# A three-layer decoder on one core: orders of latent values and context, a second bank for values, and layer 2's first steps moved into layer 1

## The reference, cut to what matters

```python
# layer 1: local attention of 16 heads of 16 (keys strictly before the query) and latent attention of 4 heads
local  = softmax(mask(q @ k.T / 4)) @ v                    # q, k, v = split(xn @ qkv_w + qkv_b)
pooled = xn.reshape(B, 64, 2, D).mean(axis=2)              # 64 latent tokens
lat    = softmax(mask(rq @ rk.T / 4)) @ rv                 # rq = xn @ rq_w + rq_b; rk, rv from pooled
remote = lat @ rout_w + rout_b
gate   = sigmoid(local @ gl_w + remote @ gr_w)             # per head
x      = x + (gate * local + (1 - gate) * remote) @ out_w + out_b
# layer 2: causal attention of x on a context
q, k, v = relu(xn @ Wq + bq), relu(ctx @ Wk + bk), relu(ctx @ Wv + bv)
x      = x + layer_norm(softmax(mask(q @ k.T / 4)) @ v + q, gamma, beta)
# layer 3: a slot feed-forward (routing to 64 slots, top 8, one GRU step, values given back)
```

## Time and profile before

| | us |
|---|---|
| median of three runs | 1517.61 |
| lowest and highest of them | 1512.31, 1517.75 |
| profiled execution | 1513.51 |
| its span | 1511.8 |

### The profile page before, as it was taken

One profiled execution on the slowest core, in us unless ns is written; L12 is line 12 of the kernel. 1 busy time (PEld: TensorE's weight loads), 2 busy tenths in 40 slices (PEclk: granted clock), 3 DMA queues, 4 the chain that ended last, 5 costly groups with the idle time before them and its releaser, 6 DMA issues. The chain is left out here.

```text
span 1511.8 us, 57218 instructions
## 1 busy us (share of the span) xinstructions
PE 1416.7 (94%) x22238; PEld 1064.8 (70%) x22238; DVE 1101.2 (73%) x3030; ACT 888.3 (59%) x1541; POOL 873.5 (58%) x1184
## 2 busy tenths in 40 slices
PE   6999999999999999985999999999999859999997
PEld 4777777777777777764777777777777636666664
DVE  6777777777777777653667676767676658989896
ACT  3555555555555555542666666666667347777773
POOL 3455555555555555542577777777777635555543
PEclk9999999999999999998999999999999969999998
DMA  5400000000000000003000000000000000010101
GB/s 165 135 2 1 0 0 0 0 0 0 0 0 0 0 0 0 2 3 120 17 24 14 21 14 21 14 21 14 21 14 8 2 1 29 29 35 28 35 28 42
DMA packets 31207, 32.40 MB, mean 21 GB/s; under 512 B 3937, under 2 KB 29602, under 8 KB 31138
## 3 DMA queue, kind: packets, MB, share of 16 engines
q1 hardware_dynamic: 31138, 31.46, 6.9%
HBM read 23.06 MB, written 8.39 MB: 21 GB/s over the span
## 5 line engine op out<-in xcount | busy, mean ns | idle before, releaser
L1028 POOL TENSOR_SCALAR_AFFINE_SELECT a_probs_t<-a_probs_t 128x512 f32<-128x512 f32 x256 | 161.9, 666 | 77.8 <-ACT a_probs_t L697 77.8
L1560 DVE TENSOR_REDUCE c_neg_max<-score_banks 128x8 f32<-128x512 f32 (+1 forms) x128 | 116.3, 950 | 80.2 <-PE score_banks L1292 80.2
L1042 POOL TENSOR_TENSOR a_less<-a_attn,a_remote 128x512 f32<-128x512 f32 x32 | 40.8, 1275 | 218.0 <-DVE a_attn L873 218.0
L1713 POOL TENSOR_SCALAR_AFFINE_SELECT c_probs_t<-c_probs_t 128x512 f32<-128x512 f32 x256 | 154.7, 639 | 12.3 <-ACT c_probs_t L1487 12.1
L1487 ACT ACTIVATE c_probs_t<-score_banks 128x2048 f32<-128x2048 f32 x64 | 120.2, 1879 | 27.2 <-PE score_banks L1320 27.2
L384 PE MATMUL side_banks<-a_xn_t,a_w_qk 128*128 128x256 f32 x512 | 134.4, 398 | 1.7 <-ACT a_xn_t L642 0.7
L697 ACT ACTIVATE a_probs_t<-score_banks 128x2048 f32<-128x2048 f32 x64 | 120.2, 1878 | 25.9 <-PE score_banks L541 25.9
L850 DVE TENSOR_REDUCE a_neg_max<-score_banks 128x8 f32<-128x512 f32 (+1 forms) x128 | 116.4, 951 | 6.0 <-PE score_banks L511 6.0
L384 PEld LDWEIGHTS side_banks<-a_xn_t,a_w_qk 128*128 128x128 f32 x512 | 93.0, 196 | 13.1 <-issue 2.4
L2141 POOL TENSOR_TENSOR r_hn<-rz_t,half_hn 128x256 f32<-128x256 f32 x32 | 23.4, 730 | 123.4 <-ACT rz_t L1970 123.4
L652 ACT ACTIVATE a_k_z<-side_banks,a_b_k,row_half 128x256 f32<-128x256 f32 x128 | 61.8, 562 | 54.0 <-PE side_banks L384 54.0
(11 more groups left out here) (263 smaller groups left out, 3927.7 us busy)
## 6 DMA issues: line engine op xcount, KB each, us to landing
x_sb<-in_x SPq DMA_DIRECT2D x32, 256.0 KB, 2.9
c_ctx_in<-in_ctx SPq DMA_DIRECT2D x32, 256.0 KB, 2.7
out<-y SPq DMA_DIRECT2D x32, 256.0 KB, 2.1
w_ih<-in_ffn_w_ih SPq DMA_DIRECT2D x1, 768.0 KB, 6.4
w_hh<-in_ffn_w_hh SPq DMA_DIRECT2D x1, 768.0 KB, 7.1
a_raw_qk<-in_attn_qk_w SPq DMA_DIRECT2D x1, 512.0 KB, 4.3
a_raw_cross<-in_xattn_qk_w SPq DMA_DIRECT2D x1, 512.0 KB, 4.7
b_ih<-in_ffn_b_ih SPq DMA_DIRECT2D x1, 384.0 KB, 6.1
```

What stands on the lines that cost most here:

```text
L1028: nc.gpsimd.affine_select(out=probs, in_=probs, pattern=[[0, 4], [1, 128]], compare_op=ALU.is_ge, fill=0.0, base=-1, channel_multiplier=-1 ...
L1560: ins = nc.vector.tensor_reduce(neg_max[:, tt, :].rearrange("p (i s l) -> p i s l", i=4, s=2)[:, :, :, late], all_scores[:, :, :, 128 * (1 ...
L1713: nc.gpsimd.affine_select(out=heads, in_=heads, pattern=[[0, 4], [1, 128]], compare_op=ALU.is_ge, fill=0.0, base=0, channel_multiplier=-1) ...
```

## The change

It has four parts. (1) In layer 1 the latent values on PE stand ahead of the second transposed scores, and on ACT `copy_lat_t` stands ahead of `evac_q`. (2) In layer 2 the second half of v goes to `q_bank`; `bias_v` is done for each half, and each half's bank is given free by itself; `project_v(at, 1)` waits for q to be evacuated. (3) In layer 2 the context is turned and copied ahead of x. (4) The loads of context pairs 0 and 1, the statistics and the norm of x's pair 0 and the statistics of pair 1 move from the head of layer 2's block into layer 1's; `v_heads` and `max_part` become tensors that both layers share, with their fixed parts set once, and layer 2's memsets go.

```diff
@@ local_attention, SyncE, behind the last loads of layer 2's weights
+            ctx = a["ctx"].rearrange("s p d -> p s d")
+            for k in range(2):
+                sp.dma_start(cross.ctx_in[k][:], ctx[:, 2 * k:2 * k + 2, :]).then_inc(cross.ctx_loaded[k], 16)
             pairs(sp, step, TAIL, ahead=2)
@@ local_attention, TensorE step
                 if prev.real:
+                    lat_values(prev)
                     scores_t(prev, 1)
-                if prev.real:
-                    lat_values(prev)
                 if at.real:
                     project_v(at, 1)
@@ local_attention, ScalarE step
                     copy_max(prev, 1)
+                    copy_lat_t(prev)
                 if at.real:
                     evac_q(at)
-                if prev.real:
-                    copy_lat_t(prev)
@@ local_attention, VectorE
+            def cross_stats(k):
+                for tt in range(2):
+                    ins = nc.vector.bn_stats(cross.stats[:, tt, :], x_rows(At(0, k), tt))
+                ins.then_inc(cross.ln_step, 1)
+                dve.wait_ge(cross.ln_step, 2 * k + 1)
+                for tt in range(2):
+                    ins = nc.vector.bn_aggr(cross.moments[:, tt, :], cross.stats[:, tt, :])
+                ins.then_inc(cross.ln_step, 1)
+
+            def cross_scale():
+                dve.wait_ge(cross.ln_scaled, 1)
...
+                ins.then_inc(cross.xn_ready, 1)
@@ step
+                if old.last:
+                    dve.wait_ge(x_done, NPAIR - 1)
+                    cross_stats(0)
+                    cross_scale()
+                    cross_stats(1)
                 if old.real:
                     add_to_x(old)
@@ local_attention, GpSimd step, behind the last mix
+                if old.last:
+                    cross_deviation(0)
+                    pool.wait_ge(cross.xn_ready, 1)
+                    cross_deviation(1)
@@ cross_attention
-    v_bank, ctxT_bank, xT_bank, maxT_bank, qT_bank = k_bank, k_bank, q_bank, av_bank, back_bank
+    v_bank, ctxT_bank, xT_bank, maxT_bank, qT_bank = (k_bank, q_bank), k_bank, q_bank, av_bank, back_bank
@@ SyncE
-            load(At(0, 0))
-            load(At(0, 1))
             slot_weights.load(sp)
@@ TensorE
             def transpose_x(at):
                 pe.wait_ge(xn_ready, at.count(1, 1))
-                wait(pe, q_ready, at.count(1, 0))
+                wait(pe, v_ready, at.count(2, 0))
...
             def transpose_ctx(at):
                 pe.wait_ge(ctx_loaded[at.par], at.turn(16, 16))
-                wait(pe, v_ready, at.count(1, 0))
+                wait(pe, v_ready, at.count(2, -1))
...
             def project_v(at, tt):
                 if tt == 0:
                     pe.wait_ge(k_ready, at.count(1, 1))
+                else:
+                    pe.wait_ge(q_ready, at.count(1, 1))
                 for c in range(C):
-                    mm = pe.matmul(v_bank[:, D * tt:D * tt + D], ctx_t[:, c, S * tt:S * tt + S], cross.w_v[:, c, :],
+                    mm = pe.matmul(v_bank[tt][:, 0:D], ctx_t[:, c, S * tt:S * tt + S], cross.w_v[:, c, :],
@@ TensorE step
                 if following.real:
+                    transpose_ctx(following)
                     transpose_x(following)
-                    transpose_ctx(following)
@@ ScalarE step
                 if following.real:
+                    copy_ctx(following)
                     copy_xn(following)
-                    copy_ctx(following)
@@ VectorE
-            def bias_v(at):
-                dve.wait_ge(v_filled, at.count(2, 2))
-                wait(dve, v_relu, at.count(1, 0))
-                nc.vector.tensor_tensor(v_raw[:], v_bank[:].rearrange("p (t d) -> p t d", t=2),
-                                        cross.b_v[:].unsqueeze(1).to_broadcast([128, 2, D]), ALU.add).then_inc(v_ready, 1)
+            def bias_v(at, tt):
+                dve.wait_ge(v_filled, at.count(2, tt + 1))
+                if tt == 0:
+                    wait(dve, v_relu, at.count(1, 0))
+                nc.vector.tensor_tensor(v_raw[:, tt, :], v_bank[tt][:, 0:D], cross.b_v[:], ALU.add).then_inc(v_ready, 1)
@@ VectorE, ahead of layer 2's steps
-            for i in range(2):
-                nc.vector.memset(v_heads[i][:], 0.0).then_inc(set_up, 1)
-            nc.vector.memset(max_part[:], 0.0).then_inc(set_up, 1)
...
-            for k in range(2):
-                x_stats(At(0, k))
-                dve.wait_ge(ln_step, 2 * k + 1)
-                x_moments()
-                if k == 0:
-                    x_scale(At(0, 0))
             pairs(dve, step, TAIL, ahead=1)
```

52 lines of the change are left out of this document (29 added, 23 removed).

## The result

The kernel after takes 1500.69 us, the median of 4 runs (1498.24 to 1501.37), beside 1515.51 us for the kernel before in the same comparison (1512.31 to 1517.75). The ratio is 0.9903 with a 95% interval of 0.9887 to 0.9919, so it is about 1% faster. In 49 runs beside the experiments the kernel before took 1511.7 to 1518.3 us (once 1521.3): under 1514.1 us with a mean granted clock of 0.978 to 0.980, above 1514.8 with 0.970 to 0.977. The profiled execution took 1500.57 us with a span of 1498.8 us, where the kernel before took 1513.51 and 1511.8: 13.0 us between the spans, against 9.2 forecast.

What follows compares the result with a forecast made beforehand. TensorE (PE), busy 94% of the span, was taken as the bound. Layer 1's order 0.9, layer 2's banks and context order 3.9 and the seam 4.4 sum to 9.2 us; from base 1515.6 that forecast 1506.4, range 1500 to 1518.

Steps and rivals of the forecast that it cites:

- 0.9 + 3.9 + 4.4 = 9.2: Gains in us forecast for layer 1's order, layer 2's banks and context order, and the seam between layers 1 and 2.
- the base of 1515.6: Whole kernel before: starting time between the profiled 1513.51 and the three-run median 1517.61, from which the gain was taken.
- rival A: Layer 2's loop keeps all 0.27 us per pair, 7.0 instead of 3.9; 12.3 in all, 1503.3 us; chance 0.13.
- 0.03 us in hand: Layer 1, latent values on PE: latent copy plus lag ready at 305.47, PE there at 305.50.
- rival C: Layer 1's latent values late by 0.35 us per pair, kernel slower at 1518.2; decides from 0.27 per pair; chance 0.10.
- The sign that the forecast named: Layer 1: latent values L461 start within 0.1 us of the end of their projection on PE.
- 0.09 us at most for L584: Layer 1: `project_out` L584 can start at most 0.09 us earlier, since L440 before it on PE ends at 311.20.
- The latent chain on DVE: Layer 1: DVE's chain from L440's end, not shortened, is next to bound; 0.03 us per pair taken from 0 to 0.13.
- 1.39 to 1.52: Layer 1: us from L576's start to L584's start expected in the profile after.
- Rival B: Layer 2's loop gives nothing, because L1347 is held already; 5.3 us in all, 1510.3; chance 0.21.
- The count of 26 pairs: Layer 2: 0.15 us gained in each of the loop's 26 pairs, 3.9 us; none taken for pairs outside the loop.
- Rival D: The seam gives half, 2.0 us instead of 4.4, by PE's low clock or slot weights' DMAs; 1508.8; chance 0.10.

Runs made afterwards that it cites:

- e7: Kernel after with ACT's old order in layer 1 (`evac_q` ahead of `copy_lat_t`), PE's new order kept; 1525.15 us, 1.0069 of the kernel before.
- e10: Kernel after with layer 1's latent transposes ahead of q's second projection and latent copy ahead of the second maxima copy; 1495.50 us, 0.9887 of the kernel before.
- e4: Kernel after with layer 2's `evac_av` moved ahead of the copy of x on ACT; 1495.39 us, 0.9866 of the kernel before.
- e6: Kernel after with x ahead of context again in layer 2 on PE and ACT, two banks kept; 1504.45 us, 0.9928 of the kernel before.
- e3: Kernel before with only the two value banks and context ahead of x in layer 2; 1510.28 us, 0.9969 of the kernel before.
- e2: Kernel before with part 4 alone (layer 2's first loads, norm and memsets moved into layer 1); 1510.22 us, 0.9966 of the kernel before.
- e1: Kernel before with part 1 alone (layer 1's new order on PE and ACT); 1509.95 us, 0.9963 of the kernel before.
- e9: Kernel after with two of the three PE waits of layer 1's latent values left out; 1499.49 us, 0.9900 of the kernel before.
- e5: Kernel after with the wait for the latent copy put last of the latent values' three PE waits; 1503.65 us, 0.9927 of the kernel before.
- e11: Kernel after with both the edits of e4 and e10; 1492.80 us, 0.9856 of the kernel before.
- e12: e11 with second scores ahead of latent values again in layer 1's last step alone; 1495.76 us, 0.9855 of the kernel before.

## Why the prediction was right, and where it was off

**The forecast's sum.** It said 0.9 + 3.9 + 4.4 = 9.2; measured between the spans are 13.0. Of the missing 3.8 us, 1.35 are layer 1's (2.25 - 0.9), 0.8 the seam and layer 2's pairs (4.52 - 4.4 and 4.59 - 3.9), and 1.64 belong to the end of layer 2 and to layer 3, where kernels without a change there differ by as much. The rest of the distance from 1506.4 to 1500.69, 1.9 us, lies between the medians and the traces: the base of 1515.6 met the median of the kernel before (1515.51), which is 2.0 above its profiled execution, while the kernel after ran at its profiled time. 1500.69 lies only 0.7 us inside the range of 1500 to 1518, below even rival A's 1503.3: the direction and the places were forecast, the size was too small in each of the three terms (11.4 us in the traces up to pair 30 of layer 2, against 9.2).

**Part 1.** The mechanism was right and its size was off. The exponential follows the scores by 0.04 and ACT is 0.44 us earlier, forecast 0.57. Two terms were mis-sized. First, the lag from ACT's copy to the latent values was taken as 0.05 and the wait to have 0.03 us in hand; it is 0.24 and 0.14, and the values start 0.14 and 0.05 late. That is rival C's place, and e7 shows that a delay there is paid in full; its point of 0.27 per pair wasn't reached. The sign that the forecast named, the values within 0.1 us of the end of their projection, came true all the same (303.19 + 1.14 = 304.33 to 304.39), since the projection's end is modelled: only the distance between the starts shows the 0.14. Second, the forecast held L440's start for PE's own turn, and so found 0.09 us at most for L584. The row it used, L440 0.73 us after L576, hid a wait: L440 waits for the copy of x, which in the kernel before ended at 309.65 + 0.61 = 310.26, 0.24 us before it. The other two things that L440 waits for were over by then (the second addition to v at 308.48 + 0.44 = 308.92), and in all traces the gap is 0.73 to 0.76 where the copy ends 0.23 to 0.27 us ahead of this line and 0.58 to 0.59 where it ends 0.67 ahead; no run moved that copy alone. With ACT earlier, L453 stands 0.59 after L589. So 0.14 us were there and 0.04 more at L597; less the late start of 0.14 and 0.05 that makes 0.04 and 0.13 in alternate pairs, and 0.04 and 0.12 were measured. The latent chain on DVE, named as what comes next, moved with L453 and held nothing. L597 starts 1.34 us after L589, outside the 1.39 to 1.52 that the prediction gave. One sum was wrong without effect: moved behind the latent copy, `evac_q` ends at 305.42 + 0.83 = 306.25, not 306.8, so 0.95 us and not 0.3 were in hand for the projection at 307.20.

That the new order of tiles costs nothing was right: e10 has 1.07 us where the old order had 1.06, and from the first projection of v to the second, over all three changes of tile, it is 2.77 in both (300.16 to 302.93, before 304.44 to 307.21). The Trainium skill, "TensorEngine Tiling (Array Packing)", section Key Properties, says that changing the tiling mode drains TensorE; with the same number of changes this gives the same sum, and the trace agrees, to 0.01 us.

**Parts 2 and 3.** 0.15 us per pair were forecast and 0.16 measured, for the reason given: L1383 starts 0.05 us after `evac_av`'s end, and e4 confirms that ACT held it. Three readings on the way were wrong, and the 0.15 didn't hang on them, since it is ACT's row that sets it. PE's order gains 0.37 us, not 0.27. `bias_v`'s second half doesn't start where the whole did, 1.33 us after the second projection, but after 1.17 (900.33 - 899.16), so x needn't wait at all (e6, where it must, shows 0.24 beyond its turn); that is where the 0.37 come from. And L1347 didn't wait for `evac_av` in the kernel before: that ended 0.20 us earlier, and PE came there only then, behind its scores. What is kept is the way from one bound to the other, 0.14 and 0.16 to 0.21 in alternate pairs. Rival A (all of PE's gain) is ruled out for the kernel after and comes true in e4, with 0.37 per pair against the kernel before. Rival B is ruled out by e3. The count of 26 pairs was too careful: all from 0 to 30 gained.

**Part 4.** 4.4 forecast, 4.52 in the pair of traces, 4.10 in e2 alone. k is projected 1.78 us after PE's first transposes of the block, forecast about 2. By the start of k's projection the lead of the seam is 4.49 us, where the forecast had 4.2; the 0.2 that it added for part 3 in the first pair didn't come (from that projection to the first exponential it is 15.79 before and 15.76 after). The memsets that went were five, not three. DVE's new instructions cost nothing: with them alone (e2) the last addition to x starts at 698.28, without them at 698.38. Rival D didn't happen by this change; but its mechanism, a low clock at the seam, did turn up by 0.8 to 0.9 us in e1 and e3.

**Rival C** had 0.10. By e7 it would have decided with ACT's order left as it was.

## What to carry to other kernels

A gap between two instructions of the bounding engine that is longer than the same gap elsewhere is a wait, even where the profile shows no idle: L440 stood 0.73 us behind four transposes and needed 0.59, and that was most of the gain in layer 1. When a wait is moved, give the one who is waited for a whole instruction's time in hand, not 0.03 us: taking that wait away in e10 earned 0.09 us per pair, as much as the reordering itself. And after each gain look once more at the in-order engine beside the bounding one: once the second bank and the new order were in, one ACT copy moved behind another (e4) was worth more, 0.20 per pair, than they had been, 0.16.

## What the hardware showed beyond expectation

- A PE instruction that waits for ACT started 0.05 us after ACT's end in most places (L1383, L597), but 0.14 to 0.25 after it at the latent values, whether PE had been idle for 0.80 us or not. L440 of the kernel before, with three waits like them, started 0.23 to 0.27 after the copy of x. Taking two satisfied waits off the latent values saved 0.10 us in one pair of two, and turning their order cost as much (e9, e5).
- On DVE something like it: `bias_v` with two waits started 1.33 us after the start of the projection, its second half with one wait 1.17. The second half also adds half as many elements. That was only compared, not varied.
- In layer 1's drain, at the seam and at layer 2's end, where PE idles for 1.8 us and more at a time, its granted clock falls to 0.5, that is from 2.4 to 1.2 GHz, in some traces and not in others with the same work there: scores of 1.17 us take 2.09, or 1.75 in part of the stretch. From the first exponential of pair 30 to the last addition to x it is 45.25 us in the kernel before, 45.91 after, 45.27 in e10, 47.35 in e11 and 50.67 in e12. That is as much as any part of this change is worth, so the parts are judged by the length of a pair in the loop and not by the whole time alone.
